# The feed-forward part's preparation and first quad in attention's last batch and drain, with staging of its own

## The reference

```python
x = L0_attn_hidden_states                                   # [8, 512, 512]
scores = jnp.einsum('bhqd,bhkd->bhqk', q, k) * scale        # q, k, v = x @ w_qkv, causal mask
attn = jnp.einsum('bhqk,bhkd->bhqd', softmax(scores), v)
x = _layernorm(x + attn @ w_o)
Wg, Wu, Wd = dequant_nvfp4(...)                             # 4-bit codes, a scale for each 32
gelu = jnp.tanh(0.7978845608028654 * (gate + 0.044715 * gate ** 3)) * gate * 0.5 + gate * 0.5
out = jnp.einsum('tn,hn->th', gelu * up, Wd)                # gate = x @ Wg.T, up = x @ Wu.T
x = _layernorm(x + out)
```

## Time and profile before

| | us |
|---|---|
| median of 3 runs | 2836.44 (2835.09 to 2837.78) |
| the profiled execution | 2834.39 |
| its span, from the first instruction to the last | 2832.6 |
| PE busy | 2716.1 (96%) |
| DVE, ACT, POOL busy | 1701.0 (60%), 1287.9 (45%), 819.9 (29%) |

### The profile page before, as it was taken

How to read it: one execution, slowest core, us unless ns; L and a number is a source line. 1 busy time by engine, 2 the same in 40 slices (tenths; PEclk the granted TensorE clock), 3 DMA queues, 4 the chain that set the end, 5 groups by cost and what they waited for, 6 DMA issues and landing times.

```text
span 2832.6 us, 38724 instructions
## 1 busy us (share of the span) xinstructions
PE 2716.1 (96%) x13314; PEld 2282.6 (81%) x13314; DVE 1701.0 (60%) x3631; ACT 1287.9 (45%) x2982; POOL 819.9 (29%) x988
## 2 busy tenths in 40 slices
PE   6999999999973999999999999999999999999998
PEld 5888888888852888888888888888888888888886
DVE  4888888888865888888633333463333354333334
ACT  4878778877753544544322222232222232222221
POOL 2444344334322443443321111141111122111112
PEclk9999999999985999999999999999999999999999
DMA  7567565755625565565544434454434336343341
GB/s 217 149 161 194 162 175 149 197 161 161 175 75 204 219 228 211 200 220 209 231 173 183 182 134 171 163 193 188 176 140 195 134 158 236 134 177 158 134 191 55
DMA packets 143092, 493.58 MB, mean 174 GB/s; under 512 B 11568, under 2 KB 48560, under 8 KB 118320
## 3 DMA queue, kind: packets, MB, share of 16 engines
q1 hardware_dynamic: 142896, 491.11, 50.6%
HBM read 356.84 MB, written 134.22 MB: 173 GB/s over the span
## 4 chain that ended last, share of the span: by engine, by line
PE 67%; DVE 1%; DMA 1%; ACT 0%; POOL 0%; issue 0%; SPq 0%; POOLq 0%; ACTq 0%; DVEq 0%
PE bank L965 22%; PE bank L966 22%; PE bank L967 22%; DMA scale<-down_scales 0%; DMA scale<-gate_scales 0%; DVE bstats L1401 0%; DMA scale<-up_scales 0%; DVE acc L1276 0%; ACT bx_h L1068 0%; DVE w_g L1249 0%; ACT wg L1068 0%; DVE bx_l L1228 0%; DVE bits L1239 0%; ACT wd L1068 0%; POOL w_sum_u L1447 0%
## 5 line engine op out<-in xcount | busy, mean ns | idle before, releaser
L1457 POOL TENSOR_TENSOR inter_l<-hid,inter_h 128x512 fp32r<-128x512 f32 x256 | 336.3, 1314 | 1363.0 <-ACT inter_h L1068 1363.0
L1276 DVE TENSOR_TENSOR acc<-acc,bank 128x512 f32<-128x512 f32 x512 | 350.3, 685 | 332.6 <-PE bank L967 324.8
L713 POOL TENSOR_SCALAR probs<-probs,row_inv 128x128 f32<-128x128 f32 (+3 forms) x512 | 263.0, 533 | 477.0 <-DVE row_inv L633 477.0
L965 PE MATMUL bank<-wd,inter_h 128*128 128x512 f32 x1024 | 399.3, 390 | 0.5 <-DVE acc L1276 0.5
L967 PE MATMUL bank<-wd,inter_l 128*128 128x512 f32 x1024 | 398.9, 390 | 0.0
L966 PE MATMUL bank<-wd,inter_h 128*128 128x512 f32 x1024 | 398.9, 390 | 0.0
L1295 DVE TENSOR_TENSOR hid<-hid,bank 128x512 f32<-128x512 f32 x192 | 132.0, 687 | 402.2 <-PE bank L967 400.5
L965 PE MATMUL bank<-bx_h,wg 128*128 128x512 f32 x896 | 350.7, 391 | 11.2 <-ACT bank L1068 11.2
L965 PE MATMUL bank<-bx_h,wu 128*128 128x512 f32 x896 | 349.7, 390 | 7.7 <-DVE wu L1260 7.7
L966 PE MATMUL bank<-bx_l,wg 128*128 128x512 f32 x896 | 350.4, 391 | 0.0
L967 PE MATMUL bank<-bx_h,wg 128*128 128x512 f32 x896 | 350.2, 391 | 0.0
(11 more groups left out here) (147 smaller groups left out, 5186.6 us busy)
## 6 DMA issues: line engine op xcount, KB each, us to landing
wg<-w_scratch SPq DMA_DIRECT2D x48, 1792.0 KB, 9.1
wu<-w_scratch SPq DMA_DIRECT2D x48, 1792.0 KB, 12.8
wd<-w_scratch SPq DMA_DIRECT2D x48, 1024.0 KB, 4.9
q_st<-qk_scratch SPq DMA_DIRECT2D x128, 256.0 KB, 5.0
k_st<-qk_scratch SPq DMA_DIRECT2D x128, 256.0 KB, 6.8
w_scratch<-wg SPq DMA_DIRECT2D x16, 1792.0 KB, 9.6
w_scratch<-wu SPq DMA_DIRECT2D x16, 1792.0 KB, 5.7
qk_scratch<-q_stage SPq DMA_DIRECT2D x32, 512.0 KB, 2.6
```

The source lines that it names most:

```text
L713: pool.tensor_scalar(p, p, row_inv[:, h % 4, k:k + 1], 1.0, ALU.mult, ALU.mult).then_inc(norm_done, 1)
L965: pe.matmul(out, a(0), b(0), start=start, stop=False, skip_group_check=True)
L1276: dve.tensor_tensor(a, a, d_bank[n % 2][:, :], ALU.add).then_inc(d_added, 1)
L1457: pool.tensor_tensor(inter[1][:, m, t, :], hid[:, 2 * m + t, :], f32(inter[0][:, m, t, :]), ALU.subtract).then_inc(inter_split, 1)
```

## The change

Attention and the feed-forward part become one block. `attention_phase` gets `feed_forward`, which returns for each engine two functions, `start(n)` and `rest()`. `start(n)` is called at the end of every slot of the last batch (n = 0 to 15) and the drain (n = 16 to 31), `rest()` after the drain; in `rest()` the quads begin with j = 1. The second block's barrier is gone. `Ends` hands over the semaphores and the counts at which attention is through with a piece of memory or a bank. The four sums of the tokens move from DVE to POOL (`first_sum`), for the first sweep only. The tiles of both parts are laid out anew, and the PSUM banks of the feed-forward part are numbered in another way. In attention's start `w_stage` has eight buffers, so no `load_w` waits.

```diff
-    w_stage = plan("w_stage", [P, 4, KC, 2 * P], F32, over="probs")
+    w_stage = [plan(f"w_stage{i}", [P, KC, 2 * P], F32, over=("probs", "a_h", "a_l")[max(i - 2, 0) // 2],
+                    skip=(i if i < 4 else i % 2) * 8 * P * KC) for i in range(8)]
+    def follow(start, b, s):
+        if b >= BATCH - 1:
+            start((b - BATCH + 1) * SLOTS + s)
             def load_w(i):
-                if i >= 4:
-                    sp.wait_ge(w_split, i - 3)
-            for i in range(6):
+            for i in range(len(PIECES)):
                 load_w(i)
-                if use in (2, 3):
-                    load_w(use + 4)
+    # sync
+        def start(n):
+            if n == 6:
+                sp.wait_ge(*ends.projected)
+                for written in ends.stacked[0]:
+                    sp.wait_ge(written, ends.stacked[1])
+                load_x(0, x_first)
+            if n == 15:
+                sp.wait_ge(x_odd, 2)
+                sp.wait_ge(x_summed, 4)
+                load_unit(0)
+                load_unit(1)
+            if n == 17:
+                load_unit(2)
+            if n == 18:
+                load_unit(3)
+            if n == 22:
+                load_unit(4)
+            if n == 25:
+                load_unit(5)
+                store_w(0, 0)
+                store_w(0, 1)
+        def rest():
+            load_acc(0, 0)
+            load_acc(0, 1)
+            for j in range(QUADS):
...
+                        if 5 < k + 3 < UNITS * NG:
+                            load_unit(k + 3)
+    # tensor
+            if n == 21:
+                wait_x(pe, 0, 0)
+                wait_split(pe, 0)
+                pe.wait_ge(*ends.values_free)
...
+                p1(0, "g")
+            if n == 22:
+                p1(0, "u")
+            if n == 23: p6(0, "g"); p2(0, "g")
+            if n == 24: p6(0, "u"); p2(0, "u")
+            if n == 25: p7(0, "g")
+            if n == 26: p5(0, "g"); p7(0, "u"); p5(0, "u")
+            if n == 27: p4(0, "g"); p4(0, "u")
+            if n == 29: p3(0, "g"); p3(0, "u")
+    # scalar: x_part at n = 8, 9, 11 to 15; then
+            if n == 16: spread(0)
+            if n == 17: spread(1)
+            if n == 18: gate_up_high(0, 0)
+            if n == 19: sums_high(0, 0)
+            if n == 20: gate_up_high(0, 1)
+            if n == 21: sums_high(0, 1); spread(2)
+            if n == 22: seed(0, "g"); spread(3)
...
+            if n == 31: split_high(0, 1, 0); spread(6)
+        def rest():
+            spread(7)
+    # vector: x_low at n = 9, 11, 13, 15; unpack(0) at 17, (1) at 18, gate_up_low(0, 0) at 19, (0, 1) at 21,
+    #   unpack(2) at 22, (3) at 23, (4) at 27, gate_up_low(1, 0) at 29, (1, 1) at 30, unpack(5) at 30 and 31
+    # gpsimd: first_sum at n = 7, 8, 10, 12, x_low at 13, 14, 15, sum_w(0, 0) at 18, (0, 1) at 20,
+    #   (1, 0) at 26, (1, 1) at 29, split_low at 28 and 31
```

More of the change, by code:

```diff
@@ L15 @@
+from dataclasses import dataclass
 import concourse.bass as bass
@@ L73, in f32, with attention_phase @@
     return ap.bitcast(F32)
-def attention_phase(nc, bank, xT_dram, x_dram, wqkvT, woT, tri, ident_dram, x1_dram, x1T_dram, qk_dram):
+@dataclass
+class Ends:
+    sbuf_end: int
+    scores_done: tuple
+    scores_masked: tuple
+    projected: tuple
+    stacked: tuple
+    values_done: tuple
+    values_free: tuple
+    outputs_free: tuple
+    transposes_free: tuple
+    x1_stored: object
+    x1T_stored: list
+def attention_phase(nc, bank, xT_dram, x_dram, wqkvT, woT, tri, ident_dram, x1_dram, x1T_dram, qk_dram, feed_forward):
     plan = Plan(nc)
@@ L123, in attention_phase @@
     const_loaded = sem("const_loaded")
-    w_loaded = [sem(f"w_loaded{i}") for i in range(4)]
+    w_loaded = [sem(f"w_loaded{i}") for i in range(8)]
     w_high, w_split = sem("w_high"), sem("w_split")
@@ L348, in body @@
                         sp.dma_start(y[:], x_dram[bass.ts(b - 1, SEQ), :].rearrange("(t p) h -> p t h", p=P)).then_inc(y_loaded, 16)
+                    follow(start, b, s)
+            start, rest = follower["sync"](sp)
             batches(body)
@@ L467, in body @@
                             transpose_x1(x1T_use(b, t, cur), t)
+                    follow(start, b, s)
+            start, rest = follower["tensor"](pe)
             batches(body)
+            rest()
         @block.scalar
@@ L565, in body @@
                         copy(a_h[:, c, :], a_sum[:, :]).then_inc(a_high, 1)
+                    follow(start, b, s)
+            start, rest = follower["scalar"](act)
             batches(body)
+            rest()
         @block.vector
@@ L691, in body @@
                         dve.tensor_scalar(var_eps[:, :], mean_var[:, :, 1], EPS, None, ALU.add).then_inc(var_done, 1)
+                    follow(start, b, s)
+            start, rest = follower["vector"](dve)
             batches(body)
+            rest()
         @block.gpsimd
@@ L720, in body @@
                                            ALU.subtract).then_inc(x_split, 1)
+                    follow(start, b, s)
+            start, rest = follower["gpsimd"](pool)
             batches(body)
+            rest()
 TILE = 512
@@ L752, with feed_forward_phase @@
 SPLIT = ((0, 0), (1, 0), (1, 1), (0, 1))
-def feed_forward_phase(nc, bank, x1_dram, x1T_dram, packed, scales, w_dram, out_dram):
+def feed_forward_phase(nc, bank, x1_dram, x1T_dram, packed, scales, w_dram, out_dram, ends):
     plan = Plan(nc)
```

982 lines of the change are left out of this document (566 added, 416 removed).

## The result

| | us |
|---|---|
| predicted | 2807.4 (2788 to 2825) |
| changed kernel, median of 4 runs | 2813.4 (2812.6 to 2814.7) |
| before, 4 runs beside them | 2837.1 (2835.1 to 2840.0) |
| ratio | 0.9919, 95% interval 0.9905 to 0.9933 |
| profiled execution, and its span | 2814.67, 2812.9 |

The change saves 24 us. I had forecast 29; the time is 6 us above the forecast and inside its range.

The account below looks back on a forecast made before the run. TensorE, busy 2716.1 of 2832.6 us, was taken as the bound, leaving only its idle time. 9.0 + 24.0 - 2.4 - 1.6 = 29.0 off 2834.39 gives 2805.4; with 2.05 for the median, 2807.4 us (2788 to 2825).

Parts of the forecast that it names:

- Start: Attention's start: the wait for w_o goes, first scores at 34.8 instead of 43.99; 9.0 us won.
- Last batch: Attention's last batch: added token preparation on ACT and DVE lengthens its slots by 6 us (2 to 11.5).
- Drain, last a_l: Drain up to the last a_l: DVE's added unpack and gate_up_low cost 8.6 us (4 to 16); it ends at 841.1.
- rival (3): Drain starved: DVE or ACT sees two more unit latencies, moving it by 15 us; 2822 us, chance 0.20.
- Last copy of x1: Attention's end: last copy at about 878.5 instead of 845.94, 32 us later (870 to 890).
- 1.6 us charged for POOL and DVE: Where POOL sums fall beside DVE work, the two get in each other's way: 1.6 us lost.
- The new wait: Turn: quad 1 waits for unit 7 behind 5.9 MB, there at 901; p6 at 904.1, 24.0 us won.
- Rival (1): Turn: queue not in issue order, unit 7 needs only 7.6 us; 6 us better, 2801 us, chance 0.15.
- Half clock after the idle time: Turn: TensorE comes back at 1.2 GHz after standing still some 18 us; 2.4 us lost.

Follow-up runs that it names:

- units_first: Changed kernel, with units 6 and 7 issued directly behind SP's wait for x1's stores, ahead of two acc loads and two weight stores; 2805.3 us (0.9886).
- start_only: Kernel before, with only the new start: eight staging buffers, all eight weight loads at once without waits; 2828.6 us, ratio 0.9966.
- turn_only: Changed kernel with the old start: four staging buffers, later weight loads waiting again; 2822.2 us, ratio 0.9946, 15.7 us faster than before.
- units_early: Changed kernel, with unit 6 issued in drain slot 12 and unit 7 in slot 15, ahead of SP's wait for x1's last stores; 2805.0 us (0.9882).

## Why the prediction was nearly right

- **Start, 9.0 taken: right by the runs.** 9.2 (6 to 13) by timing. The scores came 8.2 us early (34.8 forecast, 35.79 measured). The first matmul came 0.8 us later than before in this trace; over the eleven with this start it lies between 10.84 and 12.18, before at 11.19, so that the eight loads at once delay it is not shown. The wait for q's store grew by 2.4 to 4.99, close to the doubling that I had named; it was 1.95 to 5.07 us over the eleven traces, and the clock fell ahead of it, behind it or not at all. In the profiled execution only 2.7 to 3.3 us of the start were left, which is one sample of this stage and not its value.
- **Last batch, 6 taken: 7.2 measured (44.51 to 51.73), up to 8.5 elsewhere.** The engines named, DVE and ACT, were the right ones. POOL's seven operations were 2.33 to 2.40 alone where I had 2.9, and 3.06 and 3.28 beside DVE.
- **Drain, last a_l 14.6 later by my terms (6 + 8.6): 14.3 measured**, with the 2.7 us of the start that this trace had: 837.40 + 2.7 - 825.78. ACT's spreads of units 0 and 1 had no long waits, so rival (3) didn't come.
- **Last copy of x1 at 878.5, without the start: 880.4 to 881** (877.71 + 2.7, and its second half). I had put most of DVE's work behind TensorE's results, but here TensorE was done first and stood for 6.58 us until the copy: DVE made four subtractions of weights ahead of it, from 871.78 to 877.12, and beside POOL's sums they took 2.1 us more than the same four shapes take alone. PE, then DVE alone and beside POOL, the same line:

```profile
878.51 0.79 PE L1046 MATMUL bank<-bx_h,wg 128*128 128x512 f32 x1 [6.58 <-DVE x_stage L726]
839.44 1.22 DVE L1417 TENSOR_TENSOR wu<-w_sum_u,wu 128x1024 fp32r<-128x1024 f32 x1
875.45 1.74 DVE L1417 TENSOR_TENSOR wg<-w_sum_g,wg 128x1024 fp32r<-128x1024 f32 x1
```

  That is the 1.6 us charged for POOL and DVE, seen in one place. To put the copy ahead of these subtractions was not tried. SP goes on at 881.49 + 2.7 = 884.2, forecast 883.5: from the copy's start it was 3.8 us and not 5.0, which happened to make up for most of the delay.
- **The new wait: the mechanism right, its size short.** TensorE idle before p6 of quad 1, ACT idle before both spreads, released by a scale, all as written. The step that failed is the sum of the bytes: I let 5.9 MB (6.0, at 1024 bytes for a KB) pass at 372 GB/s and had unit 7 in 17.5 us. It took 22.5 (881.49 to 904.02). Windows of this stretch, its start and its rest:

```profile
881.49:885.60 4.11, 3.85 (x12) 2.95 (x12) 2.94 (x6) 0.00 (x0) 0.00 (x0) 0.69 0.70 195
885.60:904.02 18.42, 0.21 (x1) 0.00 (x0) 2.41 (x4) 0.63 (x2) 2.81 (x4) 0.64 0.98 365
```

  Apart from the first 4 us, at 195 GB/s, the rate, 365, was near the one that I had taken. But 7.5 MB moved in all, 1.5 more than I had counted. By the sizes of the packets in the trace these are transfers issued behind unit 7: 223 packets of 14336 bytes had started, where the store of wg has 128, so 95 (1.4 MB) were of the store of wu, and a few more of unit 8. They passed between 898.6 and 904.0, mixed with unit 7's own. At 372 GB/s they are 4.0 us, and the slow first 4 us cost 2.0. Here the queue did not finish one transfer before the next. Rival (1), that a short transfer isn't held by what stands ahead in the queue, is refuted: ahead of the long ones it took 9.3 us from its first issue (`units_first`), behind them 17.9 (886.11 to 904.02).
- **Half clock after the idle time, 2.4 charged: right.** From p6 of quad 1 to the end of the span it is 2812.9 - 906.95 = 1905.95 us; before, from 928.71, it was 1903.9, so 2.1 us more. `start_only`, with the old turn, has 1904.0, and the seven other traces that still have the new wait 1905.2 to 1906.8.

The sum: 29.0 less 5.0 for unit 7 and 0.7 for what lies ahead of SP's wait leaves 23, against 24 measured. `turn_only` puts that place on the turn alone: 15.7 where I had 20.0. One slip in the sum is small beside this: p6 of quad 1 stood at 928.71 before, not 928.3, so that 904.1 wins 24.6 and not 24.0.

This bears on the second rule of the Trainium skill that I had leaned on, "DMA: Bandwidth & Descriptors", section "Two DMAs through the same engine are not ordered", by which descriptors of one queue start in order. `units_first` and the changed kernel agree with it: unit 7 came 9.3 and 17.9 us after its issue. What the trace adds is that the store issued behind unit 7 was under way for 5 us before unit 7 had landed.

## What to carry to other kernels

When work is pulled into an earlier stage, its transfers are pulled into an earlier and fuller stretch of the queue: add up the bytes from the point where the queue goes on to the transfer that is needed first, add some of what is issued right behind it and shares the engines with it, and put the small ones that an engine waits for ahead of the large ones that nobody does. After each wait removed, ask again what is late next; here it was the seed, then the accumulator, then the next unit, all beside full DMA engines. And a stage in which TensorE stands still in pieces can't be judged from one profile, of before or after, since where the clock falls differs from run to run.

## What was not expected

- The same start, in eleven profiles, left head 3 between 3.3 and 7.9 us early. The two lowest, 3.3 and 3.5, are the two in which the granted clock fell in 50 to 54 (0.65 and 0.61, 1.00 in the others). The other nine lie between 5.3 and 7.9; over them the first matmul of all starts between 10.84 us (7.9) and 12.18, so part of the spread was there before any projection.
- A DVE subtraction of 128x1024 with both inputs in SBUF took 1.22 us alone and 3.25 beside one of POOL, which grew from 2.37 to 3.04.
- SP's issue of two scale loads took 1.28 us in a quiet queue and 4.13 in the changed kernel's full one, and the issue of one store of 1792 KB 7.36 us in `units_early`.
